# Values and ones in one strip for a weighted sum, and an inverse root by Newton steps on GpSimd

## What is computed

```python
def _layernorm(x, axis=-1, eps=1e-05):
    m = jnp.mean(x, axis=axis, keepdims=True)
    v = jnp.var(x, axis=axis, keepdims=True)
    return (x - m) / jnp.sqrt(v + eps)
...
        q_l = q.reshape(B, H, M, denom, HS).sum(axis=-2) / denom
        k_l = k.reshape(B, H, M, denom, HS).sum(axis=-2) / denom
        s1 = jax.nn.softmax(jnp.einsum('bhld,bhmd->bhlm', q, k_l), axis=-1)
        s2 = jax.nn.softmax(jnp.einsum('bhmd,bhnd->bhmn', q_l, k_l), axis=-1)
        s3 = jax.nn.softmax(jnp.einsum('bhmd,bhld->bhml', q_l, k), axis=-1)
        z_star = moore_penrose_pinv(s2, ITERS)
        out = s1 @ (z_star @ (s3 @ v))
```

## Time and profile before

| | |
|---|---|
| median of 3 runs | 1254.76 us (1254.54 to 1256.27) |
| the profiled execution | 1255.86 us, its span 1253.8 us |
| TensorE busy | 1144.5 us, 91% |
| VectorE busy | 746.6 us, 60% |
| ScalarE busy | 611.1 us, 49% |
| GpSimd busy | 530.5 us, 42% |
| mean granted TensorE clock | 0.968 of full speed |

### The profile page before, as it was taken

How to read it: one execution, slowest core, us unless ns; L and a number is a source line. 1 busy time by engine, 2 the same in 40 slices (tenths; PEclk the granted TensorE clock), 3 DMA queues, 4 the chain that set the end, 5 groups by cost and what they waited for, 6 DMA issues and landing times.

```text
span 1253.8 us, 29588 instructions
## 1 busy us (share of the span) xinstructions
PE 1144.5 (91%) x11156; PEld 931.3 (74%) x11157; DVE 746.6 (60%) x1392; ACT 611.1 (49%) x970; POOL 530.5 (42%) x535
## 2 busy tenths in 40 slices
PE   7899889999996588899999999989999889999997
PEld 5787678888885367677777777767887678888786
DVE  5536356666773555756667575565436347666664
ACT  5333246666664345454454544425443235666663
POOL 2222535666664322324323242233312534765664
PEclk9899899999999699999999999999999899999999
DMA  7173124222110300000000000010552213221220
GB/s 236 34 301 136 52 72 149 66 70 68 60 59 32 117 3 2 2 2 2 3 2 2 3 4 2 2 36 3 202 184 74 63 48 135 62 66 60 69 64 21
DMA packets 42029, 80.44 MB, mean 64 GB/s; under 512 B 9012, under 2 KB 33719, under 8 KB 40896
## 3 DMA queue, kind: packets, MB, share of 16 engines
q1 hardware_dynamic: 28640, 53.62, 12.1%
q0 software_dynamic: 13280, 25.27, 6.7%
HBM read 57.21 MB, written 27.15 MB: 67 GB/s over the span
## 4 chain that ended last, share of the span: by engine, by line
PE 70%; DVE 15%; ACT 7%; issue 5%; DMA 1%; POOL 1%; another core or an unknown queue 0%; DVEq 0%; SPq 0%; ACTq 0%; POOLq 0%
PE PS L1553 16%; PE PS L1567 10%; PE PS L1479 10%; PE PS L1496 6%; PE PS L1743 3%; PE PS L1634 3%; PE PS L1756 3%; PE PS L1560 3%; DVE A_NM L700 2%; PE PS L1503 2%; PE PS L1416 2%; DVE A_NM L707 1%; PE PS L1703 1%; PE PS L1777 1%; PE PS L1678 1%
## 5 line engine op out<-in xcount | busy, mean ns | idle before, releaser
L1553 PE MATMUL PS<-WHL,XGH 128*128 128x512 f32 x624 | 216.9, 429 | 3.4 <-DVE WHL L592 3.4
L1334 POOL TENSOR_TENSOR A_A<-A_XC,A_ST 128x320 f32<-128x320 f32 (+1 forms) x96 | 74.6, 792 | 192.0 <-ACT A_ST L1109 191.5
L1567 PE MATMUL PS<-WD,XNT 128*128 x624 | 149.9, 383 | 1.5 <-ACT XNT L1043 1.5
L613 DVE SCALAR_TENSOR_TENSOR XNT<-PS,WHO,XNT 128x512 f32<-128x512 f32 x78 | 58.3, 748 | 123.1 <-PE PS L1553 102.0
L1262 POOL DMA_INDIRECT X<-xs_dram,WHO x78 | 107.1, 1373 | 51.5 <-issue 26.4
L1553 PEld LDWEIGHTS PS<-WHL,XGH 128*128 128x128 f32 x624 | 111.3, 189 | 22.2 <-issue 2.7
L1038 ACT ACTIVATE XNT<-PS,WHO 128x512 f32<-128x512 f32 x78 | 53.7, 688 | 148.1 <-PE PS L1553 142.4
L1567 PEld LDWEIGHTS PS<-WD,XNT 128*128 128x128 f32 x624 | 112.6, 190 | 15.9 <-issue 2.0
L1496 PE MATMUL PS<-SDH,HHL 128*128 128x256 f32 x512 | 106.1, 291 | 18.8 <-DVE X L539 16.8
L1553 PE MATMUL PS<-WHL,XGL 128*128 128x512 f32 x312 | 123.1, 395 | 0.0
L1257 POOL DMA_INDIRECT who_dram<-TOK,SLOT x64 | 65.9, 1030 | 132.1 <-issue 61.6
(11 more groups left out here) (244 smaller groups left out, 2599.7 us busy)
## 6 DMA issues: line engine op xcount, KB each, us to landing
xs_dram<-WG SPq DMA_DIRECT2D x16, 512.0 KB, 2.9
WU<-in_r_up SPq DMA_DIRECT2D x2, 4096.0 KB, 13.9
shared_dram<-X SPq DMA_DIRECT2D x16, 512.0 KB, 3.1
WG<-in_r_gate SPq DMA_DIRECT2D x2, 4096.0 KB, 16.8
WD<-in_r_down SPq DMA_DIRECT2D x4, 2048.0 KB
X<-in_x SPq DMA_DIRECT2D x8, 512.0 KB, 8.8
X<-mid_dram SPq DMA_DIRECT2D x8, 512.0 KB, 3.8
X<-xs_dram,WHO POOLq DMA_INDIRECT x78
```

What stands on the lines that cost most here:

```text
L613: dve.scalar_tensor_tensor(B["RH"][:, u * F:(u + 1) * F], banks[3 + u][:], score(t), B["RS"][:, u * F:(u + 1) * F], ALU.mult, ALU.mult).th ...
L1334: pool.tensor_tensor(a, x, st, ALU.add).then_inc(att["a"], 1)
L1553: ins = pe.matmul(banks[bank][:], tok, w[:, k * F:(k + 1) * F], start=(k == 0 and i == 0), stop=(k == KD - 1 and i == 2))
L1567: ins = pe.matmul(banks[7][:, 0:D], B["HT"][:, u * F + f * P:u * F + (f + 1) * P], B["WD"][:, bass.ds(ex * (KF * D) + f * D, D)], start=(f ...
```

## The change

**The weighted sum.** V gets, for each head and token tile, a strip of 32 columns: 16 of values and 16 of ones. `pv` has one matmul for each head, with the head's own 64 columns of E3 as the moving side; values and row sums come out of the same matmul. The second head's result lies in columns 64 to 127 of the same bank, so after one transpose per c both are where TM needs them. V takes all of the old weights' place; NUM gets a buffer of its own, one of the two KBD buffers moves behind X, and WHO becomes one buffer for both feed-forwards. The ones are set once, by GpSimd, in the first period.

**The root.** For batches 1 to 7, VectorE adds epsilon, negates the mean and makes the seed of the inverse root (on the bits of the variance) right behind the aggregation. GpSimd does three Newton steps and the product with the mean, 14 operations on 128 × 4, each waiting for the one before, between `chain_a(b, 3)` and `chain_a(b, 4)`. Batch 0 keeps the old way.

```diff
             def batch_aggregate(g):
                 wait_alone(res["stat"], g * GT + GT)
+                if g > 0:
+                    wait_alone(att["xn"], count("xn", g - 1, GT))
                 for j in range(GT):
                     dve.bn_aggr(B["LNA"][:, j * 2:(j + 1) * 2], STATS[:, j * 6:(j + 1) * 6]).then_inc(res["agg"], 1)
-
-            def batch_scale(g):
-                dve.wait_ge(res["sd"], g + 1)
+                if g > 0:
+                    mean, var = (B["LNA"][:].rearrange("p (t c) -> p t c", c=2)[:, :, i] for i in range(2))
+                    wait_alone(res["agg"], aggregated(g))
+                    dve.tensor_scalar(var, var, EPS, None, ALU.add).then_inc(res["agg"], 1)
+                    dve.tensor_scalar(mean, mean, -1.0, None, ALU.mult).then_inc(res["agg"], 1)
+                    wait_alone(res["agg"], aggregated(g) + 1)
+                    dve.tensor_scalar(B["LNR"][:].bitcast(I32), B["LNA"][:].bitcast(I32).rearrange("p (t c) -> p t c", c=2)[:, :, 1],
+                                      -0.5, float(ROOT_SEED), ALU.mult, ALU.add).then_inc(res["agg"], 1)
...
-                for i, h in enumerate(HALF):
-                    dve.tensor_tensor(B["TM"][h, :].rearrange("p (c a d) -> p c a d", c=KD, d=HS), turned[h, :, 0, :, i * HS:(i + 1) * HS],
-                                      B["RDEN"][h, :].rearrange("p (c a) -> p c a", c=KD).unsqueeze(3).broadcast_to([M, KD, PC, HS]),
-                                      ALU.mult).then_inc(att["tm"], 1)
+                dve.tensor_tensor(B["TM"][:].rearrange("p (q d) -> p q d", d=HS), turned[:, :, 0:HS],
+                                  B["RDEN"][:].unsqueeze(2).broadcast_to([P, PAIRS, HS]), ALU.mult).then_inc(att["tm"], 1)
...
-                if exists(ln):
-                    batch_scale(ln)
+                if ln == 0:
+                    first_scale()
...
-                act.copy(B["V"][:, jj * 512:(jj + 1) * 512], banks[6][:]).then_inc(att["v_sb"], 1)
+                act.copy(B["V"][:, jj * 1024:(jj + 1) * 1024].rearrange("p (n w) -> p n w", w=2 * HS)[:, :, 0:HS],
+                         banks[6][:].rearrange("p (n d) -> p n d", d=HS)).then_inc(att["v_sb"], 1)
...
-                act.copy(B["TT"][:, c * 2 * P:(c + 1) * 2 * P], banks[6 + c][:, 0:2 * P]).then_inc(att["tts"], 1)
+                act.copy(B["TT"][:, c * P:(c + 1) * P], banks[6 + c][:, 0:P]).then_inc(att["tts"], 1)
...
-                if exists(ln):
-                    batch_deviation(ln)
+                if ln == 0:
+                    first_deviation_of_batches()
...
+            def batch_root(g):
+                mean, v = (B["LNA"][:].rearrange("p (t c) -> p t c", c=2)[:, :, i] for i in range(2))
+                y, t = B["LNR"][:], B["LNT"][:]
+                done = [rooted(g - 1)]
+
+                def then(ins):
+                    done[0] += 1
+                    ins.then_inc(res["rstd"], 1)
+                    pool.wait_ge(res["rstd"], done[0])
+
+                pool.wait_ge(res["agg"], aggregated(g) + 3)
+                then(pool.tensor_scalar(v, v, -0.5, None, ALU.mult))
+                for _ in range(ROOT_STEPS):
+                    then(pool.tensor_tensor(t, y, y, ALU.mult))
+                    then(pool.tensor_tensor(t, t, v, ALU.mult))
+                    then(pool.tensor_scalar(t, t, 1.5, None, ALU.add))
+                    then(pool.tensor_tensor(y, y, t, ALU.mult))
+                pool.tensor_tensor(B["LNM"][:], mean, y, ALU.mult).then_inc(res["rstd"], 1)
...
                 chain_a(b, 3)
+                if exists(ln) and ln > 0:
+                    batch_root(ln)
                 if b == PERIODS[0]:
                     for i in range(1, 4):
                         low_weights(i)
+                    wait_alone(s_low, 4)
+                    pool.memset(B["V"].rearrange("p (n w) -> p n w", w=2 * HS)[:, :, HS:], 1.0).then_inc(s_zero, 1)
                 chain_a(b, 4)
...
             def pv(b, c):
                 for j in range(GT):
-                    for a in range(PC):
-                        e3 = B["E3"][:, a * GW + j * P:a * GW + (j + 1) * P]
-                        pe.matmul(banks[6 + c][rows32(a), 0:P], B["V"][:, j * D + c * P + a * 32:j * D + c * P + (a + 1) * 32], e3,
-                                  start=(j == 0), stop=(j == GT - 1), skip_group_check=True)
-                    for a in range(PC):
-                        e3 = B["E3"][:, a * GW + j * P:a * GW + (j + 1) * P]
-                        ins = pe.matmul(banks[6 + c][rows32(a), P:2 * P], const("ones")[:, 0:32], e3,
-                                        start=False, stop=(j == GT - 1), skip_group_check=True)
+                    for i in range(2):
+                        for a in range(PC):
+                            at = ((j * KD + c) * PC + a) * 2 + i
+                            ins = pe.matmul(banks[6 + c][rows32(a), i * M:(i + 1) * M], B["V"][:, at * 2 * HS:(at + 1) * 2 * HS],
+                                            B["E3"][:, a * GW + j * P + i * M:a * GW + j * P + (i + 1) * M],
+                                            start=(j == 0 and i == 0), stop=(j == GT - 1), skip_group_check=True)
                 ins.then_inc(att["pv_ready"], 1)
...
-                for n in range(2 * KD):
-                    ins = pe.transpose(banks[7][:, n * P:(n + 1) * P], B["TT"][:, n * P:(n + 1) * P], ident)
+                for c in range(KD):
+                    ins = pe.transpose(banks[7][:, c * P:(c + 1) * P], B["TT"][:, c * P:(c + 1) * P], ident)
```

More of the change, by code:

```diff
@@ L43 @@
 EPS = 1e-5
+ROOT_SEED = 0x5f3759df
+ROOT_STEPS = 3
+ROOT_OPS = 2 + 4 * ROOT_STEPS
 CONSTS = [("ident", P), ("before", P), ("ones", P), ("halves", P), ("eye2", M), ("row_pair", 2), ("half_cols", 2),
@@ L237, in attention_buffers @@
             B[name] = b(name, cols, F32R)
-        B["TT"], B["WS"], B["BSEL"] = (X[:, NT * D + at:NT * D + end] for at, end in ((0, 2 * D), (2 * D, 3 * D), (3 * D, 4 * D)))
+        B["TT"], kbd1, B["WS"], B["BSEL"] = (X[:, NT * D + at:NT * D + at + D] for at in (0, D, 2 * D, 3 * D))
         B["E1"], B["E3"] = XNT[:, 0:PAIRS * GW], XNT[:, PAIRS * GW:PAIRS * GW + PC * GW]
         assert PAIRS * GW + PC * GW <= ROUTED_W
-        B["V"], B["NUM"] = (ATT_W[:, i * KD * GW:(i + 1) * KD * GW] for i in range(2))
-        for name, cols, dt, n in (("XTH", KD * GW, F32R, 2), ("XTL", KD * GW, F32R, 2), ("QT", KD * GW, F32, 3), ("QTR", KD * GW, F32R, 2), ("KBD", KD * P, F32, 2),
+        B["V"] = ATT_W
+        for name, cols, dt, n in (("XTH", KD * GW, F32R, 2), ("XTL", KD * GW, F32R, 2), ("QT", KD * GW, F32, 3), ("QTR", KD * GW, F32R, 2), ("KBD", KD * P, F32, 1),
                                   ("S2", 512, F32, 2), ("XC", KD * CW, F32, 2), ("MR", PAIRS * 2, F32, 2)):
             B[name] = [b(f"{name}{q}", cols, dt) for q in range(n)]
+        B["KBD"].append(kbd1)
+        B["NUM"] = b("NUM", KD * GW)
         return B
@@ L265, in emit, with aggregated, rooted @@
     PERIODS = range(-3, NG)
+    def aggregated(g):
+        return GT + g * (GT + 3) - (3 if g else 0)
+    def rooted(g):
+        return 2 + g * ROOT_OPS
     def exists(*batches):
@@ L1074, in attention_scalar, with first_deviation_of_batches @@
             B = ab
-            def batch_deviation(g):
-                act.wait_ge(res["agg"], g * GT + GT)
-                act.wait_ge(att["xn"], count("xn", g - 1, GT))
+            def first_deviation_of_batches():
+                act.wait_ge(res["agg"], aggregated(0))
                 act.activation(B["LNR"][:], B["LNA"][:].rearrange("p (t c) -> p t c", c=2)[:, :, 1], ACT.Sqrt, bias=const("eps")).then_inc(res["sd"], 1)
@@ L1804, in attention_tensor @@
                 if exists(old):
-                    pe.wait_ge(att["tm"], count("tm", b, 2))
+                    pe.wait_ge(att["tm"], count("tm", b, 1))
                     pe.wait_ge(att["xo"], count("xo", old - 2, 2))
@@ L1879, in attention_tensor @@
                     pe.wait_ge(att["e3"], count("e3", nxt, 2))
+                    if b == -1:
+                        pe.wait_ge(s_zero, 4)
                     pv(nxt, 0)
@@ L1950, in attention_tensor @@
                     turn_nm1(nxt)
-                    pe.wait_ge(att["tm"], count("tm", nxt, 2))
+                    pe.wait_ge(att["tm"], count("tm", nxt, 1))
                     pe.wait_ge(att["x"], count("x", b, 2 * PINV_ITERS))
```

17 lines of the change are left out of this document (10 added, 7 removed).

## The result

After takes 1237.49 us (median of 4 runs, 1235.17 to 1237.70); before, measured beside it, 1255.51 (4 runs, 1254.54 to 1258.97). The ratio is 0.9831, 95% interval 0.9805 to 0.9858. The forecast was 1238.3. The profiled execution took 1237.70 us with a span of 1235.9: 17.9 us less span than before, against a sum of 16.5. So the total is right; whether its terms are is the subject of what follows.

The account below looks back on a forecast made before the run. TensorE, busy 91%, was taken as the bound, with the attention's chain through both weighted sums and VectorE's tail. 13.0 + 2.2 + 1.5 + 0.6 − 0.8 = 16.5 us off 1254.76 gave 1238.3 us, range 1234 to 1242, chance 0.57.

Parts of the forecast that it names:

- Weighted sums: Attention's sums on TensorE: 64 moving columns for 128 save 0.81 us each, 13.0 us over 16 (0 to 13.9).
- smaller edits: Fewer transposes of the sums on TensorE and narrower copies of them: nothing gained, since VectorE ends the wait there.
- Rival 1: Feed limits weighted-sum matmuls to 25 to 27 ns a record; 1249 to 1251 us; chance 0.22 with its middle case.
- A_TM: Two VectorE multiplies become one, saving 0.31 us on the chain in seven batches, 2.2 us.
- The root: Layer norm, batches 1 to 7: VectorE saves 0.25 us in six batches (1.5), ScalarE 0.15 in four (0.6).
- GpSimd: The root's 14 operations take 5.0 us (2.5 to 8.8), covered by idleness before the fifth addition: no cost.
- Rival 3: GpSimd's root holds the chain's fifth addition beyond 8.6 us; at 1.0 us a step 1265 us, slower; chance 0.05.
- The three operations on VectorE: Behind the aggregation, some 0.6 us before 1.27 us idle; a GpSimd addition may hold them, using some 0.4 us beyond.
- The values' copy: ScalarE's copy of the values into strided runs of 16: between −0.1 and +0.6 us, taken as 0.
- Rival 4: The strided copy of the values doubles while the feed is at its limit: 1256 us, no change; chance 0.05.
- The start: GpSimd's memset of the ones delays VectorE's copies and the first normalisation: 0.8 us lost (0 to 1.2).
- The clock: Rival: five more batch borders run at TensorE's lower clock, costing 8.8 us, total 1247 us; chance 0.11.

Follow-up runs that it names:

- strips_only: The changed kernel with before's layer norm root; strips, single A_TM multiply and memset stay: 1240.56 us, ratio to before 0.9852, undisturbed period 51.54 us.
- tm_halves: The changed kernel with A_TM's multiply split into two halves of the partitions again: 1230.42 us (one run), undisturbed period 51.58 us against 51.26.
- narrow: The changed kernel with weighted-sum matmuls cut to 32 and 16 moving columns, results wrong: 1236.11 us (one run), undisturbed period 50.54 us.
- root_only: The kernel before with only the new root on VectorE and GpSimd; sums and A_TM as before: 1251.75 us, ratio to before 0.9934, period 53.30 us.
- after_again: The changed kernel, unchanged, run again for a second profile: 1236.74 us, ratio to before 0.9831.
- ones_later: The changed kernel with GpSimd's memset of the ones moved behind the first batch normalisation: 1241.50 us, ratio to before 0.9859.

## Why the prediction was right, step by step

- **Weighted sums.** Right, a little small: a sum became 0.85 us shorter, 0.81 forecast. By the periods of strips_only and tm_halves it is 0.91, which holds 0.06 from the smaller edits that the forecast put at nothing: 14.6 us in 16 sums in place of 13.0. The rotation of 56 ns was forecast as 58, but partly by luck: from rows whose level had another cause (narrow). Rival 1, the feed at 25 to 27 ns a record, is refuted: 14 ns is sustained in after, 9 in narrow. The Trainium skill, TensorE: Matmul & The Clock Gate, section "Wait — 56ns, not 53.3ns?", has a floor of about 25 ns from start to start; on four column groups these traces don't agree, starts lie 6 to 7 ns apart. So they do in the sums of before (5 to 7 ns between the groups of a rotation). The sentence of the prediction that before's trace does not refute the rule was a misreading: a mean of 27 ns over the engine is no distance between starts.
- **A_TM.** 0.31 us a period, shown by itself.
- **The root.** 0.37 us a period by root_only; forecast 0.25 on VectorE and 0.15 on ScalarE. Sum of both over six batches 2.2 against 2.1.
- **GpSimd.** Hidden, as forecast; 0.29 us a step, not 0.36, so 3.96 us and not 5.0. The cover is the forecast's 7.0 us (3.96 + 3.03). Rival 3 is real in kind and decides later than I put it.
- **The three operations on VectorE.** As forecast, held by a GpSimd addition and hidden. The row of the first and those behind it in after:

```profile
628.55 0.71 DVE L682 TENSOR_SCALAR A_LNA<-A_LNA 128x4 f32<-128x4 f32 x1
...
629.98 0.96 DVE L834 RECIPROCAL A_REC<-PS 128x128 f32<-128x128 f32 x1
...
632.80 0.89 DVE L818 SCALAR_TENSOR_TENSOR A_XC<-PS,A_A 128x320 f32<-128x320 f32 x2 [1.87 <-PE PS L1797]
```

  The 1.27 us idle ahead of the reciprocal are used up, the 1.86 ahead of the next A_XC are untouched.
- **The values' copy.** No loss: 0.60 us long, as before, and 0.50 of it on the chain at 636.87. Rival 4 is out.
- **The start.** −0.8 forecast, −0.77 measured.
- **The clock.** The rival that I priced at +8.8 us has the right mechanism and went the other way: 4.8 us of the attention's gain are left over when the other terms are taken off (23.0 + 0.8 − 14.6 − 2.2 − 2.2). I put them down to lower-clock places that after no longer has. The periods bear out some 4 of them. Three of before's lie in its first, fourth and sixth period. The first two gained 1.2 and 1.7 us more than the 2.41 of an undisturbed one, and the sixth 1.2 more than the fifth (neither has a root). Nothing in my rows could have told the sign, and in after_again the attention gained only 18.3.
- **Missing from the sum.** 1.7 us ahead of the attention, spread over its length. That is within what this stage scatters: in strips_only, ones_later and after_again, on one chip, it takes 401.6 to 405.1 us. Then 3.4 us behind it, of which about 3 are the fetch inside the store. They cancel the clock's gift: 19.0 − 0.8 + 4.8 − 5.1 = 17.9.

So 16.5 and 17.9 agree better than the step-by-step account deserves: terms of −5 and +5 us were not foreseen, and that they cancel is luck. The terms of the change itself are right one by one.

## What to carry to other kernels

When small matmuls rotate over column groups, halving their moving columns about halved the rotation here, from 128 columns to 64 (109 to 56 ns) and to 32 (32 ns), and no further at 16. Don't take a level from rows with another tiling. A gain read from an undisturbed period can be trusted to a few hundredths of a microsecond. But in a long program an edit also shifts the phase of the clock and the place of the instruction fetches; the first moved 4 to 5 us here, the second 3. So compare period by period before you credit the edit. A helper's long root on an idle engine is free only beside full work: check the prologue, where the same operations may be the chain.

## What the hardware did that I had not expected

- One instruction packet of 16,384 bytes inside a store of 512 packets stretched it from 1.6 to between 2.75 and 3.5 us, and the wait of the gather behind it from 9.5 to between 10.8 and 11.5 us.
- GpSimd's dependent operations on 128x4 take 0.20 to 0.23 us and follow each other in 0.29.
- Starts of matmuls in different column groups lie 5 to 7 ns apart; a sum of 64 records ran at 9 ns a record whether 32 or 16 columns moved, and at 14 with 64.
- With nothing but 223 fulfilled waits ahead of it, an unchanged attention ran three full borders at 1.2 GHz where one did (one profile of it, two of before).
